# Rows dispatched to the experts on a pitch of 576 bytes instead of 516

## The reference

```python
x = L0_attn_x                                   # (4, 1024, 128)
xn = _layernorm(x, axis=-1)
x = x + L0_attn(xn) + L0_ffn(xn)                # causal rotary attention; top-1 experts, 512 slots each
xn = _layernorm(x, axis=-1)
x = x + L1_attn(xn) + L1_ffn(xn)                # gated causal long convolution; top-2 experts
```

```python
xs = xm[tok_idx]                                # rows in the order of their experts
for e in range(E):
    h = jax.nn.relu(xs @ W1[e] + b1[e]); ye = h @ W2[e] + b2[e]
    y = y + (e_sorted == e)[:, None] * ye
out = zeros.at[tok_idx].add(y * p_sorted[:, None])
```

## Time and profile before

| | |
|---|---|
| time of three runs, us | 572.16, 575.92, 577.34 (median 575.92) |
| profiled execution, span from first to last instruction | 571.5 us |
| profiled execution's own time | not listed beside the three |
| busy in the span | PE 67%, DVE 53%, POOL 50%, ACT 35% |
| memory traffic over the span | 50.27 MB, mean 88 GB/s |
| transfers of SP and ACT: packets, MB, share of 16 engines | 56704, 36.92, 27.6% |
| indirect transfers of POOL: packets, MB, share | 6400, 12.50, 6.7% |

### The profile page before, as it was taken

The page is one execution under the profiler, slowest core; times in us unless marked ns, Lnnn a source line. Parts: engine busy times, 40 slices in busy tenths (PEclk is TensorE's granted clock), DMA queues, the critical chain, the costliest instruction groups (busy, mean ns, idle before and its releaser), DMA issues.

```text
span 571.5 us, 8121 instructions
## 1 busy us (share of the span) xinstructions
PE 381.8 (67%) x2228; PEld 303.4 (53%) x2228; DVE 304.7 (53%) x807; ACT 200.2 (35%) x501; POOL 285.8 (50%) x283
## 2 busy tenths in 40 slices
PE   2583886129698887885994943159977788787700
PEld 0451545028367556685983721137866688677600
DVE  4967593014454486535989920121356576565454
ACT  2461321015133226642220000013665556556351
POOL 2835047732646377501487777720255554565443
PEclk9997998559899699998798975559998889888955
DMA  9999938131221211100001321212122222222084
GB/s 260 383 163 160 189 98 212 55 81 27 75 64 39 65 38 37 38 1 1 5 24 42 108 69 51 69 60 74 35 65 67 72 71 60 72 74 62 10 296 145
DMA packets 63305, 50.27 MB, mean 88 GB/s; under 512 B 7314, under 2 KB 58200, under 8 KB 63006
## 3 DMA queue, kind: packets, MB, share of 16 engines
q1 hardware_dynamic: 56704, 36.92, 27.6%
q0 software_dynamic: 6400, 12.50, 6.7%
q10 hardware_dynamic: 158, 0.33, 0.3%
HBM read 26.18 MB, written 24.22 MB: 88 GB/s over the span
## 4 chain that ended last, share of the span: by engine, by line
PE 31%; DVE 12%; issue 10%; ACT 3%; DMA 2%; ACTq 1%; DVEq 1%; another core or an unknown queue 0%; SPq 0%; POOL 0%; POOLq 0%
PE psS L1054 14%; PE psO L1054 12%; PE psT L1054 2%; PE psT L1323 1%; DMA work<-moe 1%; ACTq L1006 1%; DVE xres L1757 1%; DVE ys L1685 1%; PE psS L1304 1%; ACT row L935 1%; ACT xsT L1016 1%; ACT work L918 0%; DVE work L1690 0%; DVE work L586 0%
## 5 line engine op out<-in xcount | busy, mean ns | idle before, releaser
L737 POOL DMA_INDIRECT slots<-row,slot x96 | 110.0, 1146 | 74.1 <-issue 55.0
L746 POOL DMA_INDIRECT moe<-ys,xs x64 | 63.7, 995 | 103.3 <-DVE ys L1735 58.4
L1054 PE MATMUL psS<-xsT,w12r 128*128 128x128 f32 x288 | 51.9, 307 | 14.6 <-ACT xsT L1016 14.3
L1009 ACT ACTIVATE w12r<-w 128x514 f32 x72 | 45.6, 633 | 34.3 <-PE psO L1054 26.0
L1054 PE MATMUL psO<-w12r,hT 128*128 128x128 f32 x288 | 50.7, 303 | 9.3 <-DVE hT L1725 4.6
L1054 PE MATMUL psS<-work 128*128 128x512 f32 (+3 forms) x96 | 41.5, 545 | 21.1 <-DVE work L1534 11.3
L1054 PEld LDWEIGHTS psS<-xsT,w12r 128*128 128x128 f32 x288 | 42.3, 211 | 20.5 <-ACT xsT L1016 18.7
L1054 PEld LDWEIGHTS psO<-w12r,hT 128*128 128x128 f32 x288 | 42.2, 211 | 12.3 <-issue 11.3
L1559 DVE SCALAR_TENSOR_TENSOR xres<-psO,work,xres 128x128 f32<-128x128 f32 x32 | 11.1, 346 | 66.0 <-remote 43.8
L1054 PE MATMUL psO<-work 128*128 128x128 f32 x288 | 40.3, 286 | 7.2 <-DVE xres L1559 4.5
L1735 DVE TENSOR_TENSOR ys<-psO,b 128x128 f32<-128x128 f32 x72 | 20.8, 289 | 42.2 <-PE psO L1054 31.4
(11 more groups left out here) (285 smaller groups left out, 869.3 us busy)
## 6 DMA issues: line engine op xcount, KB each, us to landing
slots<-xs SPq DMA_DIRECT2D x13, 516.0 KB, 14.3
xs<-slots SPq DMA_DIRECT2D x64, 64.5 KB
work<-moe SPq DMA_DIRECT2D x8, 512.0 KB, 4.0
xres<-in_x SPq DMA_DIRECT2D x4, 512.0 KB, 9.3
mats<-in_fw SPq DMA_DIRECT2D x1, 2048.0 KB, 11.3
moe<-xs SPq DMA_DIRECT2D x4, 512.0 KB, 7.4
mats<-in_iv SPq DMA_DIRECT2D x8, 256.0 KB, 2.9
xT<-moe SPq DMA_DIRECT2D x4, 512.0 KB, 8.6
```

The costliest lines, as they stand in the source:

```text
L737: pool.indirect_dma_start(dst[:, :], bass.IndirectOffsetOnAxis(ap=slots[:, i:i + 1], axis=0), row[:, i, :], None, bounds_check=bound, oob_ ...
L746: pool.indirect_dma_start(dst[:, :], bass.IndirectOffsetOnAxis(ap=row_slots[l][m][:, D:ROWW].bitcast(I32), axis=0), ys[:, n % UNROLL, :], ...
L1009: act.activation(w12r[:, n % W_RING, :], w12[:, bass.ds(e, 1), :].rearrange("p e h -> p (e h)"), ACT.Copy).then_inc(e_w1, 1)
L1054: return pe.matmul(o, lhsT, rhs, start=start, stop=stop)
```

## The change

A row gets 144 columns instead of 129: 128 values, the number, and 15 columns of padding (zeros in `row`, and 1 << 24 in the fill, where only the first is read). A row is now 576 bytes long, and since rows lie one behind the other in the slots, they begin at multiples of 576 bytes instead of 516. Every transfer of rows carries all 144 columns. POOL has one more instruction, which clears the padding once (`pad_done`). To make room, `stats` shares the memory of `xsT`, the scratch area shrinks, and `tile_no` is kept once and not eight times, so `cst` is 504 columns shorter (1336 instead of 1840).

```diff
-ROWW = D + 1
+PAD = 16
+ROWW = D + PAD
...
-                    ("carry", E * NT), ("decay", J), ("minus_half", J), ("tile_no", TILES1 * E),
+                    ("carry", E * NT), ("decay", J), ("minus_half", J), ("tile_no", TILES1),
...
-    put("tile_no", np.repeat(np.arange(TILES1), E))
+    put("tile_no", np.arange(TILES1))
...
-        stats = sb("stats", [P, NT, 6])
...
         xsT = sb("xsT", [P, 2, P])
+        stats = xsT[:, :, :].rearrange("p n q -> p (n q)")[:, 0:NT * 6].rearrange("p (i s) -> p i s", s=6)
...
-        WORK = 17200
+        WORK = 17128
...
+            pool.memset(row[:, :, D + 1:ROWW], 0.0).then_inc(pad_done, 1)
             pool.wait_ge(cst_loaded, 16)
-            ids = row[:, :, D:ROWW].rearrange("p i w -> p (i w)").bitcast(I32)
+            ids = row[:, :, D:D + 1].rearrange("p i w -> p (i w)").bitcast(I32)
...
-                    dst[:, :], bass.IndirectOffsetOnAxis(ap=row_slots[l][m][:, D:ROWW].bitcast(I32), axis=0),
+                    dst[:, :], bass.IndirectOffsetOnAxis(ap=row_slots[l][m][:, D:D + 1].bitcast(I32), axis=0),
...
             pool.wait_ge(ids_done, 1)
+            pool.wait_ge(pad_done, 1)
             pool.wait_ge(prefilled, 16 * N_FILL)
...
             rstep(tt(ecmp[:, :, :], ctile[0:1, :].unsqueeze(1).to_broadcast([1, TILES1, E]),
-                     cst[0:1, CONST["tile_no"][0]:CONST["tile_no"][1]].rearrange("p (n e) -> p n e", e=E), ALU.is_le))
+                     cst[0:1, CONST["tile_no"][0]:CONST["tile_no"][1]].unsqueeze(2).to_broadcast([1, TILES1, E]), ALU.is_le))
```

More of the change, by code:

```diff
@@ L400, in two_layer_kernel @@
         ids_done = sem("ids_done")
+        pad_done = sem("pad_done")
         stats_done = sem("stats_done")
```

## The result

The changed kernel takes **575.8 us** (median of 20 runs, 568.7 to 580.7), the kernel before 570.1 us in the same measurement (20 runs, 563.8 to 580.1). The ratio is 1.0103, with an interval of 1.0068 to 1.0137: 1% slower. My forecast was 557 us. Ratios leave out the runs that lie over 1.5% above their kernel's fastest, which of the widely spread kernel before leaves the quicker part, so a ratio can lie above that of the medians of all runs, which I give beside it.

A forecast was written before the change was run, and what follows sets the result against it. No engine is busy throughout; the fills set layer 0's scatter start, and a stall of PE, DVE and ACT follows. Fills (19.2 us) and constants (0.8) bring its end 20 us forward, taken as 19: 575.9 - 19 = 557 us, range 552 to 583.

The forecast's parts named there:

- The fills: Layer 0's slot fills: from 161 to 326 GB/s, 42.7 to 23.5 us, 19.2 us less before the first scatter.
- The 0.8 us for the shorter constants: 504 fewer constant columns ahead of the inputs: 0.26 MB less, moving the scatter's start 0.8 us earlier.
- The other end of my bound: Layer 0's fills staying at 161 GB/s with rows of 576 bytes: 47.6 us, 5.0 more.
- rival (c): Layer 0's fills don't speed up: 575 to 580 us, chance 0.22.
- Where the stall sets in: Layer 0: at the same burst of hspec products as before, so it ends 20 us earlier; 19 us taken as gain.
- rival (a): Layer 0's stall sets in at about 70.7 and takes the gain back: 571 to 578 us, chance 0.20.
- rival (b): Layer 0's stall from 70.7 lets nothing through the three engines: 7 to 10 us slower, 583 to 586, chance 0.10.
- my price of (a): Layer 0's earlier stall loses 25 to 29 us, against about 27 before: no change.
- Unchanged terms: Scatters at 0.97 us each, loads on the path and layer 1's stall: nothing changes, layer 1's stall only 20 us earlier.
- Rival (d): Crooked scatters cause the stall, which goes: 27 us less in layer 0, 15 in layer 1, 534 us, chance 0.08.
- my sum: Whole kernel: layer 0's scatter starts at 57.2 us and 19 us are gained, span 571.5 to 552.5.

The follow-up runs named there:

- The ladder: Three kernels on one chip with the stall: changed kernel unchanged 575.9 us, its first scatter held to the fifth bias value 568.4, to the sixth 578.0.
- e8_after_again: The changed kernel once more, unchanged, on a chip without the stall: 500.3 us, one execution.
- e14_held5_ladder: The changed kernel with layer 0's scatter held until DVE's fifth bias value: 568.4 us (12 runs), ratio 0.9995 to the kernel before.
- e1_held: The changed kernel with layer 0's scatter held until DVE's sixth bias value: 578.6 us (6 runs), ratio 1.0191 to the kernel before.
- e3_pace1: The changed kernel with POOL waiting in layer 1 after every 8 scatters until they landed, layer 0 unbroken: 567.5 us (12 runs), ratio 0.9990.

## Why the prediction was wrong

**The fills: right in kind, 5 us too high.** I took 326 GB/s and a start of the scatter at 57.2. It is 303 GB/s, and 62.0 (60.8 in two other executions). Of the 4.8 us, 7.67 MB at 303 instead of 326 GB/s are 1.8, and in the profiled execution the fills began 2.3 us later (16.2, not 13.9). In the other executions of such rows they begin at 13.3 to 14.9, so that part is chance. The 0.8 us for the shorter constants show in no trace: the fills of the kernel before begin at 13.9 to 14.4. The other end of my bound, 5 us more, is out, and rival (c) with it.

**Where the stall sets in: the step that failed.** I let it set in "at the same burst of products with hspec as now", since 6.4 matmuls a us in the stretch at 63 to 71 lay between the 4.3 at which nothing stalled and the 8.9 ahead of the stall. It set in there. That is rival (a), to which I gave 0.20: stall from about 70, 8.4 us of PE's work done in it (I had some 5 to 9), no gain. The ladder shows the step by itself: with the start behind that stretch the stall comes at 91 and the scatter's earlier end is a gain of 5 us at tile 8; with the start ahead of it all is lost. My measure was poor too: I compared rates of matmuls, and 6.4 a us did not pass. What sets the stall off stays open. It isn't each hand-over from PE: in the kernel before, with the scatter running since 77.2, ACT still gets PE's work on time,

```profile
80.65 0.60 ACT L928 ACTIVATE work<-psT 128x512 f32<-128x512 f32 x1 [0.75 <-PE psT L1158]
...
89.17 0.60 ACT L928 ACTIVATE work<-psT 128x512 f32<-128x512 f32 x1 [5.04 <-PE psT L1158]
```

the second after the same wait as where nothing stalls (5.03 us, `e8_after_again`). What may set that time apart is that DVE has work of its own throughout (12.6 of 12.7 us, 15.8 of 15.9 in `e14_held5_ladder`), which was my reason in rival (b); no experiment tests it.

**What it costs: my price of (a) was right in the trace, rival (b)'s sign was right in the median.** The two profiled executions have the same span. The medians lie 5.7, 3.8 and 5.7 us apart in three measurements. From the ladder, a start at 77.2 us (that of before) would, by my estimate, between 72.1 (568.4) and 80.1 (578.0), give 574.5, and the changed kernel has 575.9. So the place of the start accounts for some 1.4 us of the 5.7. The rest stays open. The profiled execution of the changed kernel lies 2.3 us under its median, and that of before was one of the longer ones, if it lies as much over its span (2.15 us) as that of the changed kernel: 573.7 against 570.1. I have no trace of the quicker executions of the kernel before where the stall shows.

**Unchanged terms.** Scatters stay at 0.97 us and 1.28 apart, loads of eight tiles take 3.69 us after 3.66. Layer 1's stall stands as predicted, though not 20 us earlier. All these were right.

**Rival (d)**, the stall comes from crooked rows, is out: rows of 576 bytes stall alike, and rows of 516 bytes don't where the chip doesn't.

**The case I did not have**: that what I took for a property of the kernel is one of the chip. Where nothing stalls, the attention rows don't care about the scatter and PE waits 10.25 us for tile 8's rows. There the change does what my sum says in kind (10.0 us at the scatter's start, 9.0 at tile 8) and is worth 4.2 us (0.8%) at the end, by one trace of each.

## What to carry to other kernels

When a step is moved to an earlier place, ask what it holds up while it runs, not only what waits for its end: here the 16.8 us won at the scatter's end were paid with two attention rows stranded behind it. Where two engines' hand-overs fail during a run of transfers, try the start at two or three places and a pause every eighth transfer before the start is taken as early as it can be, and time it on more than one chip: the pauses gave 2.4% where the stall shows and cost the kernel before 1.5% where it doesn't. Rows that are written one behind the other should start at multiples of 32 bytes; rows of 516 bytes that start at multiples of 4 took 41.7 to 48.9 us here, and rows of 544 and 576 some 34.

## What the runs showed of the hardware

**A stall that some chips have.** During layer 0's unbroken run of GpSimd's indirect transfers PE's finished work isn't noticed by DVE and ACT for up to 34 us (34.5 in `e1_held`), and the last such wait ends some 4 us behind the last transfer (3.2 to 4.5). That the signal is held up, and not the work, is only argued, from the kind of wait: the longest waits of the changed kernel of that kind,

```profile
ACT work L998 <- remote: 40.2, 2, 29.5
...
DVE hT L1689 <- remote: 28.8, 2, 28.0
```

(what waited for what, us in total, times, longest), against the longest of ACT and DVE on the chip without the stall, where no wait of the whole program names such a release:

```profile
DVE hT L1729 <- PE psS L1058: 45.5, 4, 42.4
ACT work L998 <- PE psT L1058: 42.3, 4, 35.4
```

(of those the 42 us are DVE's wait for layer 1's rows, and in the 35 us, from 263 to 298.6, DVE is busy for 32 and ACT isn't needed). So a long wait of ACT in layer 1 isn't all stall: `e3_pace1`, whose layer 1 is paced, has one of 37.0 us there that names no release either. The stall isn't confined to the two scatters. The experts of layer 1, with transfers back in short runs, take 135.5 us in the changed kernel,

```profile
400.40:535.90 135.50, 110.73 (x787) 99.90 (x788) 78.62 (x207) 83.73 (x224) 68.27 (x68) 0.94 0.23 65
```

and 110.7 us without it, for the same 787 matmuls. In all the kernel before takes 64 to 74 us more on the chips with the stall; that the stall is the whole of it is not shown, and its fills are slower in the one trace of it there. What in the chip or its state makes the difference no run here shows.

**Fills.** 13 x 1024 rows with starts at multiples of 4 bytes were handed over in 48.9 us (161 GB/s) in the one trace with the stall and in 41.7 us (190 GB/s) on the two chips without it; with starts at multiples of 32 or 64 they took 33.0 to 34.0 us in every trace, with 516, 544 or 576 bytes a row.
